# Fewer transposes in an attention block: quotients taken in the transposed layout, queries from x transposed by the host

## The reference

```python
x = x + tanh(g_xattn) * xattn(layernorm(x), ctx, pos, pos, Wq, Wkv, Wout, bout)
x = x + tanh(g_ffn) * ffn(layernorm(x), gate_w, up_w, down_w, expert_weight, gamma, beta)
# xattn: 32 heads of 16
q = rope(layernorm(x) @ Wq);  k, v = split(ctx @ Wkv);  k = rope(k)
w = softmax(q @ k.T / 4);     out = (w @ v) @ Wout + bout
# ffn
y = relu(h @ up_w) ** 2 @ down_w + (h @ expert_weight) * (sum of the two largest of h @ gate_w)
out = layernorm(y) * gamma + beta
```

## Time and profile before

| | |
|---|---|
| median of 3 runs | 1601.75 us (1600.06 to 1601.91) |
| the profiled execution | 1600.03 us, its span 1598.2 us |
| PE, DVE, ACT, POOL busy | 97%, 61%, 40%, 19% of the span |
| TensorE clock granted | 0.991 in the mean |
| opening | 0 to 63.4 us |
| iteration 0 | 63.4 to 104.9 us |
| iterations 1 to 13 | 104.9 to 688.6 us, 44.9 us each |
| iteration 14, 15 | to 725.3 us, to 760.7 us |
| phase 2 | 760.7 us to the end |

### The profile page before, as it was taken

How to read it: one execution, slowest core, us unless ns; L and a number is a source line. 1 busy time by engine, 2 the same in 40 slices (tenths; PEclk the granted TensorE clock), 3 DMA queues, 4 the chain that set the end, 5 groups by cost and what they waited for, 6 DMA issues and landing times.

```text
span 1598.2 us, 26049 instructions
## 1 busy us (share of the span) xinstructions
PE 1542.5 (97%) x9818; PEld 1157.1 (72%) x9818; DVE 976.6 (61%) x1448; ACT 638.5 (40%) x962; POOL 295.7 (19%) x370
## 2 busy tenths in 40 slices
PE   8799999999999999988999999999999999999997
PEld 6466666666666666655787887888878878788886
DVE  7887777878877777865662535436444354353524
ACT  3365555555655555566442222222222222222221
POOL 5212222222221222201010201002011020010202
PEclk9799999999999999999999999999999999999999
DMA  6644444445544334433530101101001011010101
GB/s 173 142 114 103 106 102 114 116 113 128 128 114 109 103 100 112 99 97 98 166 114 1 54 27 33 38 11 53 27 27 33 21 48 33 12 48 21 50 4 40
DMA packets 67192, 121.24 MB, mean 76 GB/s; under 512 B 12280, under 2 KB 25720, under 8 KB 67064
## 3 DMA queue, kind: packets, MB, share of 16 engines
q1 hardware_dynamic: 67064, 119.50, 27.9%
HBM read 51.17 MB, written 16.78 MB: 43 GB/s over the span
## 4 chain that ended last, share of the span: by engine, by line
PE 84%; DVE 11%; issue 2%; ACT 1%; POOL 1%; DMA 0%; POOLq 0%; DVEq 0%; ACTq 0%; SPq 0%
PE pP L986 16%; PE pA L1183 11%; PE pO L986 11%; PE pB L1183 11%; PE pT L986 9%; PE pO L1108 6%; PE pA L1080 6%; DVE mneg L1402 5%; PE pM L986 4%; PE pB L1096 2%; PE pT L993 2%; PE pP L993 2%; PE pM L993 2%; PE pM L1150 1%; DVE xn L1291 1%
## 5 line engine op out<-in xcount | busy, mean ns | idle before, releaser
L1402 DVE TENSOR_REDUCE mneg<-pA 128x4 f32<-128x1024 f32 x250 | 305.6, 1222 | 136.4 <-PE pA L1080 134.6
L887 ACT ACTIVATE probs<-pB 128x1024 f32<-128x1024 f32 x249 | 255.2, 1025 | 257.8 <-PE pB L1096 247.6
L1505 DVE TENSOR_TENSOR relu<-relu 128x512 f32<-128x512 f32 x128 | 88.4, 691 | 250.2 <-ACT hid L939 250.1
L704 POOL TENSOR_SCALAR var_eps<-meanvar 128x1 f32<-128x1 f32 x96 | 34.5, 360 | 1039.3 <-DVE meanvar L1287 1039.1
L1183 PE MATMUL pA<-dn,hid 128*128 128x512 f32 x768 | 196.9, 392 | 1.2 <-DVE hid L1507 1.0
L1183 PE MATMUL pB<-dn,hid 128*128 128x512 f32 x768 | 195.0, 389 | 0.0
L986 PE MATMUL pP<-fT,up 128*128 128x512 f32 x768 | 188.5, 394 | 0.0
L986 PE MATMUL pO<-fT,up 128*128 128x512 f32 x768 | 185.0, 390 | 0.0
L1183 PEld LDWEIGHTS pA<-dn,hid 128*128 128x128 f32 x768 | 143.0, 188 | 33.8 <-DVE hid L1507 4.5
L986 PEld LDWEIGHTS pO<-fT,up 128*128 128x128 f32 x768 | 143.9, 188 | 30.5 <-issue 0.5
L1183 PEld LDWEIGHTS pB<-dn,hid 128*128 128x128 f32 x768 | 144.2, 188 | 30.0
(11 more groups left out here) (199 smaller groups left out, 1972.8 us busy)
## 6 DMA issues: line engine op xcount, KB each, us to landing
stk<-kT SPq DMA_DIRECT2D x180, 128.0 KB, 2.9
stq<-qT SPq DMA_DIRECT2D x180, 128.0 KB, 3.0
fres<-x_scratch SPq DMA_DIRECT2D x34, 256.0 KB, 2.8
xin<-x SPq DMA_DIRECT2D x32, 256.0 KB, 3.0
xres<-x SPq DMA_DIRECT2D x32, 256.0 KB, 3.2
x_scratch<-xres SPq DMA_DIRECT2D x32, 256.0 KB, 2.3
out<-y_s SPq DMA_DIRECT2D x32, 256.0 KB, 2.0
fx<-x_scratch SPq DMA_DIRECT2D x29, 256.0 KB, 2.7
```

Source lines behind the costliest of these rows:

```text
L704: nc.gpsimd.tensor_scalar_add(var_eps[:], meanvar[:, 1:2], EPS).then_inc(ve_made, 1)
L887: nc.scalar.activation(probs[:, s % 4, :, :, :].rearrange("p a b s -> p a (b s)"), psum[:, :, :], ACT.Exp).then_inc(exp_done, 1)
L1402: nc.vector.tensor_reduce(mneg[par][:, :, 2 * u:2 * u + 2].rearrange("p t q -> p q t"), psum[:, :, :].rearrange("p q (t k) -> p q t k", t= ...
L1505: nc.vector.tensor_tensor(r[:], r[:], r[:], ALU.mult).then_inc(sq_made, 1)
```

## The change

Four parts.

1. **Quotients.** Jobs a00 to a11 and aT0, aT1 go, with their evacuations. Now `av_s` stays in its transposed layout. DMAs gather the denominators of a half of the heads (`gather_den`, 1 DMA of 16 KB) into a tile of 64x64; DVE takes their reciprocals and splits them (`reciprocals`, 3 operations, half 0 in step 14, half 1 in step 3 of the next iteration); `scatter_recips` (2 DMAs) lays them out as 32 rows; new jobs b0 and b1 (2 matmuls each with a matrix of ones and zeros) spread each reciprocal over the 16 rows of its head; meanwhile `move_av` (4 DMAs) compacts the products into `numer`, DVE multiplies, ACT rounds (`round_av`), POOL takes the rest (`rest_av`). Wout's rows are permuted on the host to fit.
2. **Queries.** For sequences 2 to 15 jobs X0 and X1 go, and DVE's `ln_apply`. x is also given transposed by the host (`xT`); `load_xT` brings it, POOL splits it (`split_x`). The mean is taken out of the weights instead (8 matmuls at the end of the opening, a copy on ACT, `centre_weights` on POOL over four chunks of Wq loaded again), and 1/sqrt(variance) goes onto the cosine and sine tables of the tile (two small operations on DVE ahead of each Q evacuation).
3. **SP's order** is written anew (below).
4. **Schedule.** V1 moves from step 11 to 4 and into bank pT; O0 and O1 are cut in halves over steps 9, 11 and 13, 15 with V0 between O1's halves.

```diff
 SCHEDULE = {
-    0: ("X0", "a10"),
+    0: (),
     1: ("K0",),
-    2: ("Q0<", "a01"),
+    2: ("Q0<", "b0"),
     3: ("m1", "Q0"),
-    4: ("a11",),
-    5: ("X1", "kT0"),
-    6: ("aT0",),
+    4: ("V1",),
+    5: ("kT0",),
+    6: ("b1",),
     7: ("K1", "Q1<"),
-    8: ("Q1", "O0<"),
-    9: ("kT1", "O0"),
+    8: ("Q1",),
+    9: ("kT1", "O0<"),
     10: ("qT0",),
-    11: ("aT1", "V1"),
+    11: ("O0",),
     12: ("m0", "qT1"),
-    13: ("O1",),
+    13: ("O1<",),
     14: ("V0",),
-    15: ("a00",),
+    15: ("O1",),
 }
+RECIPROCALS = {14: 0, 3: 1}
+ROUNDED = {4: 0, 8: 1}
 # SP
+            def gather_den(b, h):
+                sp.wait_ge(av_taken, GROUPS * b + GROUPS // 2 * (h + 1))
...
+                sp.dma_start(den[:, :], av_s[HD:P:32, GROUPS // 2 * h:GROUPS // 2 * (h + 1), :]
+                             .rearrange("j g (r s) -> j (g r) s", r=4)).then_inc(den_in, INC)
+            def scatter_recips(b, h):
+                n = 2 * b + h
+                sp.wait_ge(rc_made, 3 * (n + 1))
...
+                for k, part in enumerate((den_hi, den_lo)):
+                    sp.dma_start(recips[NH // 2 * k:NH // 2 * (k + 1), :].bitcast(F32), part[:, :].bitcast(F32)).then_inc(rc_in, INC)
+            def move_av(b, h):
...
+                for j in range(MOVES):
+                    sp.dma_start(numer[j:P:4, 2 * h:2 * h + 2, :].rearrange("p c s -> p (c s)"),
+                                 av_s[32 * j:32 * j + HD, GROUPS // 2 * h:GROUPS // 2 * (h + 1), :]
+                                 .rearrange("d g s -> d (g s)")).then_inc(moved[h], INC)
 # SP, iteration, the order after the change
+                if within(bt):
+                    move_av(bt, 0)
+                if ending:
+                    first_loads()
                 if within(b1) and not opened("kT1", b1):
                     load_stack(b1, (par + 1) % 2, 1, "k")
+                if within(bt):
+                    gather_den(bt, 1)
+                if within(b2):
+                    load_xT(b2, 1)
+                if within(bt - 1):
+                    store_x1(bt - 1, 1)
+                if within(bt):
+                    move_av(bt, 1)
+                    scatter_recips(bt, 1)
+                if within(i):
+                    load_max(i, par % 2, 1)
+                if within(bt):
+                    load_residual(bt)
+                if within(b1) and not opened("kT1", b1):
                     load_stack(b1, (par + 1) % 2, 1, "q")
                 if within(i + 3):
                     load_x(i + 3, 0)
+                    load_xT(i + 3, 0)
                     load_x(i + 3, 1)
                     load_ctx(i + 3)
+                gather_den(i, 0)
...
+                if within(b2):
+                    load_stack(b2, par % 2, 0, "k")
                 if within(bt):
                     store_x1(bt, 0)
                 if within(b1):
                     load_max(b1, (par + 1) % 2, 0)
                 if within(b2):
                     load_stack(b2, par % 2, 0, "q")
+                scatter_recips(i, 0)
 # POOL
+            def rest_av(b, h):
+                pool.wait_ge(at_hi, 2 * b + h + 1)
+                cut = slice(2 * h, 2 * h + 2)
+                nc.gpsimd.tensor_tensor(aT_lo[:, cut, :], numer[:, cut, :], aT_hi[:, cut, :].bitcast(F32),
+                                        ALU.subtract).then_inc(at_lo, 1)
+            def split_x(b, t):
...
+                nc.gpsimd.tensor_copy(xnT[0][:], xv).then_inc(xT_split, 1)
+                pool.wait_ge(xT_split, 2 * n - 1)
+                nc.gpsimd.tensor_tensor(xnT[1][:], xv, xnT[0][:].bitcast(F32), ALU.subtract).then_inc(xT_split, 1)
 # DVE, evacuation of Q
+                    if name[0] == "Q" and not opened(name, b):
+                        dve.wait_ge(rstd_made, n + 1)
...
+                        for side in (cos_t, sin_t):
+                            own = side[:, n, :, :, :].rearrange("p w k l -> p (w k l)")
+                            nc.vector.tensor_scalar(own, own, rstds[t][:, 0:1], None, ALU.mult).then_inc(scaled, 1)
+            def reciprocals(b, h):
+                n = 2 * b + h
+                dve.wait_ge(den_in, INC * (n + 1))
...
+                nc.vector.reciprocal(d, d).then_inc(rc_made, 1)
+                dve.wait_ge(rc_made, 3 * n + 1)
+                nc.vector.tensor_copy(den_hi[:, :], d).then_inc(rc_made, 1)
+                dve.wait_ge(rc_made, 3 * n + 2)
+                nc.vector.tensor_tensor(den_lo[:, :], d, den_hi[:, :].bitcast(F32), ALU.subtract).then_inc(rc_made, 1)
 # DVE, step: maxima, evacuations of the step before, LN statistics, then
+                    if s in RECIPROCALS and within(i - RECIPROCALS[s]):
+                        reciprocals(i - RECIPROCALS[s], RECIPROCALS[s])
 # PE
+                    pe.wait_ge(rc_in, 2 * INC * (2 * b + t + 1))
+                    for c in range(2):
+                        last = nc.tensor.matmul(psum[:, c * S:(c + 1) * S], spread[:, c, :], recips,
+                                                start=True, stop=True)
```

More of the change, by code:

```diff
@@ L109 @@
 CUT = [x[:-1] for names in SCHEDULE.values() for x in names if x[-1] == "<"]
-TWO_STEP = ("X0", "X1", "qT0", "qT1", "kT0", "kT1", "aT0", "aT1", "m0", "m1")
+TWO_STEP = ("X0", "X1", "qT0", "qT1", "kT0", "kT1", "m0", "m1")
 ROPES = ("K0", "Q0", "K1", "Q1")
-A_JOBS = ("a00", "a10", "a01", "a11")
+R_AT = HALF_ROWS
+R_ROWS = 2 * NH // 2
+MOVES = 4
 X_AT = (6, 8, 10, 12)
@@ L219, in sb1, with under @@
             return first.enter_context(nc.sbuf_tensor(name, shape, dt))
+        def under(name, shape, dt=F32):
+            with nc.sbuf_tensor(name, shape, dt) as tile:
+                return tile
         wq_s = [sb1(f"wq{i}", [P, KC, D], F32R) for i in range(2)]
@@ L628, in _ @@
             load_ctx(2)
+            load_xT(2, 0)
+            sp.wait_ge(*done_of("kT1", 1))
+            sp.wait_ge(w_lo, KC - 2 + CC)
+            for c in range(KC):
+                sp.dma_start(raw_again[c], chunks[CC + c][0]).then_inc(w_again[c], INC)
             for x in "kq":
@@ L727, in iteration @@
                 if prepares:
-                    inv_std(b2 * TT + 2)
+                    inv_std(b2 * TT + 2, 1)
                     rope_sum(b2, "K0")
+                if within(bt):
+                    rest_av(bt, 0)
+                if prepares:
+                    rope_sum(b2, "Q0")
+                    split_x(b2, 1)
                 if within(bt):
@@ L1032, in opening @@
                         job(value, -1, -1)
+                pe.wait_ge(mean_w_made, 1)
+                for c in range(KC):
+                    for w in range(2):
+                        last = nc.tensor.matmul(pO[:, :], mean_w[:], wq_s[w][:, c, :],
+                                                start=(c == 0 and w == 0), stop=(c == KC - 1 and w == 1))
+                last.then_inc(col_done, 1)
                 pe.wait_ge(o_taken, len(OPENING))
@@ L1206, in fblock @@
                     if first_block and m == 0:
-                        job("a01", B, B)
                         pe.wait_ge(gt_lo, 1)
@@ L1464, in _ @@
             phase1(dve, iteration, ahead=1)
-            job("a00", B - 1)
+            job("O1", B - 1)
             split_gate()
-            job("a10", B)
             dve.wait_ge(av_done, GROUPS * B)
```

255 lines of the change are left out of this document (176 added, 79 removed), and 12 rows, old and new, of tables (BANK, LAG).

## The result

| | before | after |
|---|---|---|
| median | 1601.2 us (4 runs) | 1678.89 us (1673.67 to 1682.92, 4 runs) |
| ratio | 1 | 1.0484, 95% interval 1.0452 to 1.0516 |
| profiled span | 1598.2 us | 1678.8 us |
| TensorE clock granted, mean | 0.991 | 0.938 |
| opening and iteration 0 | 104.9 us | 106.7 us |

Iteration 14 of the kernel before began at 688.41 us (its first `logits_a`), not at 688.60 as I had it, so it took 36.9 us and not 36.7. Phase 2 after the change is counted from its first product with up's weights (837.80); before, from the transposes 0.56 us ahead of that product.

A forecast was written before the change was run, and what follows sets the result against it. PE was taken to bound full iterations and phase 2. Terms 13 x -1.8 = -23.4, +0, +5, +0, -1.3 gave -19.7 us; against the 1601.75 us median 1582, taken as 1581 us, range 1548 to 1602.

The forecast's parts named there:

- rival B: SP's queue becomes the bound, by small DMAs ahead of step 3's reciprocals; decides from a 3.3 us wait; 1619 us; chance 0.13.
- PE's work in a full iteration, at full clock: Iterations 1 to 13: falls from 43.9 to 40.3 us, eight transpose groups removed and b0, b1 added at 0.5 us.
- PE's idle time in it: Full iterations: 0.9 us from steps 0, 5 and 9, plus DVE's 1.9 us wait for the denominators.
- PE's time lost at half clock: Full iterations: no loss in the sum; a fall of PE's clock in the new gaps was listed as proving it wrong.
- iteration 14: No change from 36.7 us: 33.9 from shorter steps, but the late gather takes 2.8 to 3.5 back.
- iteration 15: +5 us on 35.4: 8 us from denominators late behind first_loads, 3 returned by missing transposes; alternatives 0 and +8.
- phase 2: First block, PE-bound: five transpose groups of 0.36 us go and two b jobs come, -1.3 us.
- The wait: Step 3: DVE waits 1.9 us for half 1's denominators, whose gather SP issues 9.2 us into the iteration.
- the price of the wait: Full iterations: the 1.9 us wait goes through whole, making 43.1 us instead of 41.2, 1.8 less than before.
- DVE's sum: Full iterations: DVE drops some 6.8 us of work and gets some 3.5, falling to 32 of 43 us.
- A: Rival: step 3's denominators are in time, full iterations gain 3.7 us each, 1552.5 us in all; chance 0.25.
- C: Rival: DVE's small operations wait for POOL's, one or two an iteration losing 1 us; 44.0 an iteration, 1594 us; chance 0.12.

The follow-up runs named there:

- Experiments 2: Changed kernel, late gather kept, with V1's matmuls made twice in step 4 and kT0's transposes three times in step 5: 1636.8 us, ratio 1.0216.
- 7: Kernel before the change, with DVE making the maxima 1 more time in step 3 into an unread tile: 1616.09 us, ratio 1.0091.
- 8: Kernel before the change, with DVE making the maxima 3 more times in step 3 into an unread tile: 1672.84 us, ratio 1.0438.
- 11: Kernel before the change, with DVE making the maxima 2 more times in step 3 into an unread tile: 1649.67 us, ratio 1.0312.
- experiment 3: Changed kernel, with half 1's gather of denominators issued ahead of the first loads of phase 2 in iteration 15 only: 1679.13 us, ratio 1.0485.
- Experiments 4: Kernel of experiment 1, with POOL making phase 2's first 1/sqrt ahead of the bias onto the residual in iteration 15: 1593.42 us, ratio 0.9946.
- 6: Kernel of experiment 5, with store, scatter, moves, maxima and residual ahead of three of up's four loads in iteration 15: 1581.61 us, ratio 0.9870.
- experiment 5: Kernel of experiment 4, with the scatter of half 1's reciprocals issued ahead of its four moves in every iteration: 1587.64 us, ratio 0.9916.
- experiment 9: Kernel of experiment 6, with POOL's bias behind the rest of half 1, and fx's DMA ahead of the moves in iteration 15: 1582.41 us, ratio 0.9887.
- experiment 12: Kernel of experiment 9, with POOL's two additions of the bias moved behind Q1's rotated sum: 1575.19 us, ratio 0.9839.
- experiment 1: Changed kernel, with half 1's gather of denominators issued right after the first four moves, ahead of stack k: 1599.71 us, ratio 0.9995.

## Why the prediction was wrong

The measured 1678.9 us is 77 us above the upper end of my range (1548 to 1602), and 60 above rival B's 1619. The sum of the prediction, put against the change's profiled span of 1678.8 us (forecast 1598.2 - 19.7 = 1578.5; against the median the same sum gives 1582, and I had no reason for taking it as 1581):

| term | forecast | measured | difference |
|---|---|---|---|
| PE's work in a full iteration, at full clock | 40.3 us | 41.0 | 13 x 0.7 = +9 |
| PE's idle time in it | 2.8 us | 3.8 | 13 x 1.0 = +13 |
| PE's time lost at half clock | 0 | 44.8 - 41.0 = 3.8 | 13 x 3.8 = +50 |
| iteration 14 | 36.7 us | 41.7 | +5 |
| iteration 15 | 40.4 us | 57.3 | +17 |
| opening, iteration 0 | 0 | +1.7 | +2 |
| phase 2 | -1.3 | +3.5 | +5 |

(44.8 is the mean of PE's busy time in the 13 windows, 3.8 what their mean of 48.6 leaves. 41.0 is PE's busy time in iteration 6, at full clock.) The sum of the differences is 101 us; 100.3 were missing.

**The wait was right, in place, cause and nearly in size.** Issue 9.2 us into the iteration forecast, 9.2 to 11.0 measured; DVE's wait 1.9 forecast, 1.63 to 3.42 measured; 0.6 us for each small DMA held (0.61 for the gather, 2.5 to 2.8 for four moves). What I had not in it was that a stack's six issues take up to 4.9 us in this queue and not 3.7. The kernel before had shown that too: its trace has stacks of 5.02 us (from 150.71) and 5.21 us (from 379.38), and the ones in the earlier trace rows are among the quick ones.

**The step that failed is the price of the wait.** I wrote that the wait "goes through whole: 43.1 us an iteration" and took an idle microsecond for a microsecond. The clock stood at the end of the prediction only, as a thing that would make it wrong, dismissed with the gaps of 1.09 us in iteration 14. But the forecast itself had 1.9 + 0.5 us of idle in two neighbouring steps, twice as much as any row that I used as evidence. Rows that spoke against me stood in the opening of the same trace, where the logits' four matmuls go from 0.50 to 0.80 us behind idles of 1.71, 1.82 and 0.63 us:

```profile
48.15 0.50 PE L1080 MATMUL pA<-stk,stq 48*128 48x256 f32 x4 [1.82 <-DVE mneg L1402]
49.29 0.80 PE L1080 MATMUL pB<-stk,stq 48*128 48x256 f32 x4 [0.63 <-DVE mneg L1402]
```

The clock fell in 12 of 13 iterations, and at 50 us it is half of the error. Experiments 2 (DVE's wait kept, PE's idle filled, clock up, 42 us less) and 7, 8 and 11 (idle alone, clock down) show it from both sides. The one iteration where it stayed up took 43.8.

**PE's work** was a term of the sum that was mis-sized, by 0.7 us: b0 and b1 cost 0.43 us each from start to start (310.14 to 310.57), 0.86 together and not 0.5; the other 0.3 I didn't trace. DVE's sum was too low as well (forecast 32 us, 34.3 in iteration 6), at no cost that the runs show.

**Iteration 15**: I chose "+5, returned by the missing transposes", with the late denominators as the cause. They were late (DVE waited 8.71 us), but experiment 3 shows that they weren't last. The step that failed is that I followed the new SP order only for the DMAs that the change adds, and not for the residual, which the kernel before issues ahead of `first_loads` and the change behind it: POOL's bias waits for it, and POOL's 1/sqrt for phase 2 stands behind the bias. Experiments 4 and 6 took 6.5 and 5 us of it away.

**Iteration 14** has the same wait (4.03 us at 751.43) and a clock of 0.75; I had it at 0. The wait isn't what first brought the clock down there: it was at 0.50 from 747.7 us on, behind idles of 1.09, 0.77 and 1.20 us, ahead of the wait. It stayed there until 768.2 us; in experiments 5, 9 and 12, with the gather early, it fell behind nearly the same three idles for 3 to 7 us. With the gather early iteration 14 took 36.4 us at a clock of 0.91 (experiment 12), so my 33.9 without the wait was too low as well.

**Phase 2** was to gain 1.3 and lost 3.5. All of it is in the first block: from the first product with up's weights to that of the second block it took 110.2 us before (761.26 to 871.50) and 113.3 after (837.80 to 951.05); the second took 102.8 in both. The change's trace shows the same mistake a third time. SP issues a load of down's weights behind a store, the gather, the residual, four moves and the scatter (839.43 to 847.46), ACT waits for it, PE waits for ACT, and PE's clock is at half from 853.5 to 856.9 us:

```profile
847.50 0.58 SPq L676 DMA_DIRECT2D y_s<-down  x1
```

```profile
850.58 0.62 ACT L1034 CAST dn<-y_s 128x512 fp32r<-128x512 f32 x1 [7.43 <-DMA y_s<-down]
```

```profile
852.97 0.39 PE L1349 MATMUL pM<-ident,fx 16*128 16x16 f32 x4 [2.09 <-ACT fx L1119]
```

No run tries another order there, and the kernel of experiment 12 still has its phase 2 at 839.4.

**The rivals.** A (no wait) is what experiments 1 and 5 made: full iterations of 42.1 us where A had 41.2, and 1587.6 in all, 35 us over A's 1552. B named the chain and the slower side, and put the point where it decides at a wait of 3.3 us (4.4 with issues of 1 us each). The waits stayed below that in 12 of 13 iterations and the small issues at 0.6 us, so B's mechanism isn't what happened; with the clock in the price, a mean wait of 2.35 was enough. C's mechanism is real: in the change it struck the cast of the denominators in five of 13 iterations (0.40 to 1.24 us instead of 0.19), in addition to the wait; in experiment 9 it alone took 0.7 us an iteration. That is near the 0.9 us that C forecast, but in the change it came in five iterations and not in each.

## What to carry to other kernels

On a bound engine whose clock is granted, price an idle twice: its length, and what the engine loses behind it at half clock; look whether the trace shows an idle of *that* length, with its neighbours, at full clock, before putting the second price at zero. When an order of DMAs is rewritten, follow each moved DMA to who waits for it and to what stands behind that waiter in its own program, not only the DMAs that are new. A wait that is removed shows the next one: here 1678.9 became 1575.2 in six steps (experiments 1, 4, 5, 6, 9 and 12), each of them a change of places in SP's queue or POOL's program, of which one (9) gained nothing by itself.

## What the runs showed of the hardware

- PE's granted clock fell from 1.00 (2.4 GHz) to 0.50 (1.2 GHz) behind a single 1.64 us in 8 of 13 iterations, and behind a single 2.77 us in 9 of 13 (in two more it fell about 6 us after it, behind shorter idles). In the change it fell behind 2.31 us alone, behind 2.31 and 1.74 us and behind 0.78 and 1.74 us; in experiment 1 behind 0.60 and 0.93 us. It stayed at 1.00 behind 0.51 and 1.74 us with 1.3 us of work between, behind one idle of 2.64 us in the first full iteration of experiment 5, and in all 13 iterations with idles of 0.51 and 0.74 us.
- An idle of 1.09 us is no safe one. In the kernel before it left the clock up, in iteration 14 as in iteration 15. In iteration 15 of the change a single one brought it down, as these rows of PE show (0.80 us for four matmuls that take 0.50 at 823.32):

```profile
786.44 0.50 PE L1271 MATMUL pA<-stk,stq 48*128 48x256 f32 x4 [1.09 <-DVE mneg L1602]
...
789.71 0.80 PE L1287 MATMUL pB<-stq,stk 50*128 50x256 f32 x4
```

- Once down, the clock stayed down with PE busy for 10 us in eleven of the change's full iterations (321 to 331 us in iteration 5), and for 3 or 7 us in those of experiments 1, 8 and 11. What decides whether an idle brings it down I can't say from the runs. The Trainium skill (TensorE: Matmul & The Clock Gate, What's actually happening) has the monitor run in its own time, whatever the kernel does; that the same 1.64 us led to a fall in only some iterations agrees with it.
- SP took 0.6 to 0.7 us to issue most DMAs of 8, 16, 64 or 128 KB from SBUF to SBUF, and about 0.4 us for the residual's 256 KB from HBM (two in 0.83 us). In different iterations of the change six of 128 KB took 3.7 to 4.9 us and four of 64 KB 2.5 to 4.4.
- A DVE operation of 0.2 us took 1.15 us (the cast at 315.98 in the change) to 1.32 us (experiment 9) beside a POOL operation of about 1.27 us that had begun with it or just before.
